# Where the output tiles of a four-layer program stand: later in three phases, earlier in the last one, with row scores of the third layer among its projections

## What is computed

```python
x = x + attn_a(layernorm(x))   # gated slot attention, 16 heads of 128: short convolutions of
                               # q, k, v, w; decays g; a scan over tokens; then
    o = o * rsqrt(mean(o * o, axis=-1) + 1e-5) * norm_w * sigmoid(gate)   # gate = h @ Wg1 @ Wg2 + bg2
    return o.reshape(...) @ Wo
x = x + ffn(layernorm(x))      # causal attention, 16 heads of 128, and 4 experts with top 2
x = x + attn_b(layernorm(x))   # full attention, 16 heads of 16
x = x + ffn(layernorm(x))      # the same weights again
```

## Time and profile before

| | us |
|---|---|
| median of 3 runs | 2605.76 |
| lowest, highest | 2604.42, 2606.11 |
| profiled execution | 2609.29 |
| its span in the trace | 2607.4 |

### The profile page before, as it was taken

How to read it: one execution, slowest core, us unless ns; L and a number is a source line. 1 busy time by engine, 2 the same in 40 slices (tenths; PEclk the granted TensorE clock), 3 DMA queues, 4 the chain that set the end, 5 groups by cost and what they waited for, 6 DMA issues and landing times. The chain is left out here.

```text
span 2607.4 us, 49048 instructions
## 1 busy us (share of the span) xinstructions
PE 2329.5 (89%) x18400; PEld 1615.0 (62%) x18400; DVE 1677.2 (64%) x3286; ACT 1191.4 (46%) x2936; POOL 1100.7 (42%) x1265
## 2 busy tenths in 40 slices
PE   7888888888888888888759999999889989999999
PEld 4577655776557865577635666676533356666685
DVE  7667686677766767677536777742357567777613
ACT  5655455554555545555324555432115535455411
POOL 0477434774347743377525544420130035444300
PEclk9999999999999999999879999998889989999999
DMA  2100001000010000000012000000100030000000
GB/s 63 37 2 3 2 17 37 2 2 2 17 37 2 2 2 17 17 3 2 2 52 74 15 19 19 7 1 1 50 1 1 1 115 19 19 19 13 1 1 17
DMA packets 57640, 46.29 MB, mean 18 GB/s; under 512 B 11576, under 2 KB 50880, under 8 KB 57024
## 3 DMA queue, kind: packets, MB, share of 16 engines
q1 hardware_dynamic: 57408, 43.16, 5.7%
HBM read 42.10 MB, written 1.05 MB: 17 GB/s over the span
## 5 line engine op out<-in xcount | busy, mean ns | idle before, releaser
L1182 DVE SCALAR_TENSOR_TENSOR work<-four,taps,work 128x511 f32<-128x511 f32 (+2 forms) x384 | 285.4, 748 | 101.6 <-ACT work L861 92.0
L1807 POOL TENSOR_TENSOR rot<-q_plain,ropes 128x512 f32<-128x512 f32 x64 | 81.0, 1266 | 577.0 <-ACT q_plain L1838 577.0
L931 ACT ACTIVATE work<-four 128x512 f32<-128x512 f32 x216 | 129.0, 597 | 270.1 <-PE four L690 243.8
L576 PE MATMUL four<-xT,wring 128*128 128x512 f32 x512 | 252.2, 620 | 0.2 <-DVE work L1182 0.2
L741 PE MATMUL four<-work 128*128 128x128 f32 x1536 | 217.2, 286 | 0.0
L1851 ACT ACTIVATE pr<-four,nmaxf 128x512 f32<-128x512 f32 (+3 forms) x256 | 134.0, 525 | 171.2 <-DVE nmaxf L1689 171.2
L1689 DVE TENSOR_REDUCE nmaxf<-four 128x1 f32<-128x512 f32 (+3 forms) x256 | 125.8, 491 | 125.7 <-PE four L1532 121.7
L741 PEld LDWEIGHTS four<-work 128*128 128x128 f32 x1536 | 193.5, 196 | 4.0
L1530 PE MATMUL four<-rot,rot 128*128 128x512 f32 (+3 forms) x512 | 179.0, 445 | 5.2 <-DVE rot L1681 3.6
L1117 POOL TENSOR_TENSOR work<-work 128x256 f32<-128x256 f32 x184 | 146.5, 796 | 77.5 <-DVE work L1263 56.1
L1124 POOL TENSOR_TENSOR work<-work 128x256 f32<-128x256 f32 x184 | 141.9, 771 | 84.0 <-PE bank L775 74.0
(11 more groups left out here) (276 smaller groups left out, 5429.3 us busy)
## 6 DMA issues: line engine op xcount, KB each, us to landing
wqkv<-in_f_wq_dram SPq DMA_DIRECT2D x32, 128.0 KB, 2.2
wqkv<-in_f_wk_dram SPq DMA_DIRECT2D x32, 128.0 KB, 2.4
wqkv<-in_f_wv_dram SPq DMA_DIRECT2D x32, 128.0 KB, 2.3
wo<-in_f_wo_dram SPq DMA_DIRECT2D x2, 2048.0 KB, 11.7
we<-in_f_we_dram SPq DMA_DIRECT2D x4, 1024.0 KB
wring<-in_Wk_dram SPq DMA_DIRECT2D x4, 512.0 KB, 3.8
wring<-in_Ww_dram SPq DMA_DIRECT2D x4, 512.0 KB, 5.5
wring<-in_Wv_dram SPq DMA_DIRECT2D x4, 512.0 KB, 3.9
```

Of the source, the lines that this page charges most:

```text
L576: last = nc.tensor.matmul(unit_bank(i)[:], wring[n % 2][:, c, h * P:(h + 1) * P], k.xT[:, c, b * T:(b + 1) * T], start=(c == 0), stop=(c = ...
L1182: ins = nc.vector.scalar_tensor_tensor(out=cbuf[i % 4][:, n:], in0=unit_bank(i)[:, 0:T - n], scalar=taps[:, {"q": 0, "k": 1}.get(kind, 2), ...
```

## The change

It has four parts, and no arithmetic is changed.

1. **Phases of groups 1 to 3.** For an output tile `turn_y` comes 4 steps after its first step (3 before), `keep_y` 5 (4), `result` 7 (5), `add` 8 (6).
2. **Last group.** Six of its 8 tiles (those whose chunks are complete; `LAST_TILES` orders them first) are issued among the levels of s = 8 and s = 9 (`LATE`, `last_outputs`): `gate` of tile e, `turn_y` of e - 1, `result` of e - 2 at place e. They use banks 0, 2, 3 and other buffers. POOL makes the roots in two parts: 24 of 32 columns at s = 8, j = 0, and 8 after the slots. Two tiles stay behind the slots.
3. **Norm statistics.** `measure` takes `bn_stats` and `bn_aggr` of a tile right after the last addition to it, in the last group of the first layer, in the last expert of the second and at the end of the third. The three blocks that follow lose theirs and wait for a counter.
4. **Third layer.** The four row scores of unit 0 follow the parts 4, 7, 10 and 13 of the projections, their maxima on DVE one part later. The projections move from banks 0 to 3 to banks 4 to 7.

```diff
@@ -144,7 +145,16 @@
+def measure(k, dve, stage, n, t=None):
+    nc, signal = k.nc, k.measured[stage]
+    t = n if t is None else t
+    nc.vector.bn_stats(k.stats[:, t, :], k.x[:, t, :]).then_inc(signal, 1)
+    dve.wait_ge(signal, 2 * n + 1)
+    nc.vector.bn_aggr(k.mean_var[:, t, :], k.stats[:, t, :]).then_inc(signal, 1)
...
+LATE = {(B * CH, j): j - 1 for j in range(1, LEVELS)} | {(B * CH + 1, 0): LEVELS - 1, (B * CH + 1, 1): LEVELS}
+LAST_TILES = [b * CH + c for b in range(B) for c in range(CH - 1)] + [b * CH + CH - 1 for b in range(B)]
+NEARLY = B * (CH - 1)
...
 (PE)
+                def last_outputs(e):
+                    gate(NG, e)
+                    if 1 <= e <= NEARLY:
+                        turn_y(NG, e - 1)
+                    if 2 <= e <= NEARLY + 1:
+                        result(NG, e - 2)
...
-                    t = token_tile(g, i - 3)
+                    t = token_tile(g, i - 4)
                     if t is not None:
                         turn_y(g, t)
                     t = token_tile(g, i)
                     if t is not None:
                         gate(g, t)
-                    t = token_tile(g, i - 5)
+                    t = token_tile(g, i - 7)
                     if t is not None:
                         result(g, t)
...
                     if g == NG:
-                        gate(g, 0)
-                        for t in range(NT):
-                            if t + 1 < NT:
-                                gate(g, t + 1)
-                            turn_y(g, t)
-                            if t:
-                                result(g, t - 1)
+                        turn_y(g, NT - 2)
+                        turn_y(g, NT - 1)
+                        result(g, NT - 2)
                         result(g, NT - 1)
                         break
...
                             if early(g, s, j) is not None:
                                 phase(g + 1, early(g, s, j))
+                            if late(g, s, j) is not None:
+                                last_outputs(late(g, s, j))
...
 (ACT)
-                    t = token_tile(g, i - 4)
+                    t = token_tile(g, i - 5)
                     if t is not None:
                         keep_y(g, t)
...
 (POOL)
+                            if g + 1 == NG and (s, j) == (B * CH, 0):
+                                pool.wait_ge(out_squared, g * SLOTS * HG + NEARLY * HG)
+                                root(NG, by_chunk(ss_o)[:, :, 0:CH - 1], by_chunk(rt_o)[:, :, 0:CH - 1], [P, B, CH - 1, HG])
+                            if late(g, s, j) is not None and late(g, s, j) < NEARLY:
+                                weigh(NG, late(g, s, j))
...
 (DVE)
+                    if g == NG:
+                        dve.wait_ge(x_added, (g - 1) * NT + t + 2)
+                        measure(k, dve, 0, t, m)
...
+                def last_outputs(e):
+                    bias(NG, e)
+                    if 1 <= e <= NEARLY:
+                        scale_y(NG, e - 1)
+                    if 2 <= e <= NEARLY + 1:
+                        add(NG, e - 2)
...
-                    t = token_tile(g, i - 6)
+                    t = token_tile(g, i - 8)
                     if t is not None:
                         add(g, t)
...
 (second layer, DVE, last expert)
+                        if n >= E * NT and rows is None:
+                            dve.wait_ge(y_used, n + 1)
+                            measure(k, dve, 1, t)
...
 (third layer)
+FIRST_ROWS = {4 + 3 * r: r for r in range(CH)}
...
+                    if i in FIRST_ROWS:
+                        pe.wait_ge(c_roped, 2)
+                        score_rows(0, FIRST_ROWS[i])
...
+                    if n - 1 in FIRST_ROWS:
+                        maximum(0, FIRST_ROWS[n - 1])
```

More of the change, by code:

```diff
@@ L169, in then @@
                 dve.wait_ge(k.norm_chain, chain[0])
[L171 to L176 removed]
+            if measured is None:
+                for t in range(NT):
+                    last = nc.vector.bn_stats(k.stats[:, t, :], src[:, t, :])
+                then(last)
+                for t in range(NT):
+                    last = nc.vector.bn_aggr(k.mean_var[:, t, :], k.stats[:, t, :])
+                then(last)
+            else:
+                dve.wait_ge(k.measured[measured], 2 * NT)
             nc.vector.tensor_scalar(k.rstd[:], k.mean_var[:, :, 1], EPS, None, ALU.add).then_inc(k.norm_var, 1)
@@ L1225, in _ @@
                     if g == NG:
-                        bias(g, 0)
-                        for t in range(NT):
-                            if t + 1 < NT:
-                                bias(g, t + 1)
-                            scale_y(g, t)
-                            if t >= 2:
-                                add(g, t - 2)
+                        scale_y(g, NT - 2)
+                        scale_y(g, NT - 1)
                         add(g, NT - 2)
@@ L2196, in _ @@
                     if n < NC_UNITS:
-                        for r in range(1, CH):
+                        for r in range(1, CH) if n else ():
                             maximum(n, r)
```

191 lines of the change are left out of this document (110 added, 81 removed).

## The result

| | before | changed |
|---|---|---|
| median of 4 runs, us | 2605.94 | 2557.40 |
| lowest, highest | 2604.42, 2606.31 | 2552.39, 2561.54 |
| profiled execution, its span | 2609.29, 2607.4 | 2561.54, 2559.8 |

The ratio is 0.9821 with a 95% interval of 0.9802 to 0.9840: 47 us faster (42 to 52). Forecast were 2560.6, or 45.2 us, in a range of 2546 to 2584.

The account below looks back on a forecast made before the run. PE, busy 89% of the span, bounds the kernel with its list plus its waits. Terms -28.5 - 2.7 - 2.45 + 2.7 - 12.4 - 1.8 = -45.2 us, giving 2560.6 us, range 2546 to 2584.

Parts of the forecast that it names:

- Part 1, forecast -28.5: Phases of groups 1 to 3: waits for `scale_y` nearly vanish, those for additions partly stay; 9.5 us gained per group.
- 3 to 6.8 us of waits are left: Phases of groups 1 to 3: of PE's 14.0 us of waits per group, this much remains after the change.
- the `scale_y` was to start ahead of POOL's weighing: In the phases, `scale_y` would start 0.3 us before POOL's weighing, which otherwise makes it 3.61 us in place of 0.68.
- Part 2, forecast -2.7: Last group: six tiles among the levels; its end with statistics at 1350.6 in place of 1353.35, bounds -10 and +15.
- Four steps of the working: Last group: chunk 7's first level +6.8 us, a level 5.6, low clock 3 for the first tile, 4.5 for the last two.
- Part 3, forecast -2.45, +2.7 and -1.8: Norm statistics: second layer's beginning gains 2.45 us, its end loses 2.7, third layer's end and fourth's beginning gain 1.8.
- Part 4, forecast -12.4: Third layer: 17.07 us less 3.9 for row scores and 2.3 for the fourth maximum, plus 1.5 from the clock; bounds -9, -15.
- what the clock gives back behind the transpose: Third layer: without the long idle stretch the clock stays up and the next two steps come 1.5 us earlier.
- Rival 1: Phases: waits for additions replace those for turns, gain 3 us per group in place of 9.5; 2580 us, chance 0.15.
- Rival 2: Last group's levels run at the lower clock, five of them adding 17.5 us; 2578 us, chance 0.12.
- Rival 3: All 14 us of waits vanish in each group and the tail runs at full clock; 2540 us, chance 0.08.
- Rival 5: Most of 32 `scale_y` meet POOL's work, 2.93 us more each; kernel slower, 2619 us from 20 of 32; chance 0.04.

Follow-up runs that it names:

- the weighing in pieces: POOL's weighing of bw cut from two instructions into eight, on the changed kernel with additions first, row scores earlier, no second-layer statistics and unread matmuls: 2528.37 us, ratio 0.9716.
- the warm end: Seven unread matmuls ahead of the last two tiles' turns in the last group, on the changed kernel: 2552.92 us, ratio 0.9809.
- part 4 alone: The kernel before with only the third layer's row scores moved among its projections, and these on banks 4 to 7: 2591.72 us, ratio 0.9958.
- additions first on the old distances: The kernel before with only the addition moved to the head of its step, turn_y 3, keep_y 4, result 5, add 6: 2601.18 us, ratio 0.9990.
- three smaller edits: On the changed kernel: row scores two parts earlier, no second-layer statistics, seven unread matmuls before the last tiles; together with additions first 2538.93 us, ratio 0.9761.

## Why the prediction came out right, point by point

**Part 1, forecast -28.5.** The mechanism was right, the size only in part. From the last projection of group 0 to the first pair of s = 8, three executions without part 1 took 1181 to 1186 us, five with it 1149 to 1158; between the means, 1183.4 and 1153.5, lie 30.0. In the waits, 9.3 + 4.7 became 4.1 + 1.3 + 0.6, which is 8.0 a group and not 9.5; PE's whole idle time fell by 22.7. The other 7.2 us are PE's busy time for the same matmuls, which the forecast had put at nothing; that fewer waits keep the clock up is likely, but not shown apart from the scatter. So that the phases came to what was forecast is partly luck. That "3 to 6.8 us of waits are left" holds (6.0). The reason given for the wait that is left, an addition of the step before, is confirmed by the edit that moves the addition to the head of its step. One point failed: the `scale_y` was to start ahead of POOL's weighing. It still meets it, at the last tile of each phase, and takes 3.21 us (3.61 before); the new wait of 1.3 us at a turn is this one, and the run with the weighing in pieces shows that it held more than that once the additions were out of the way.

**Part 2, forecast -2.7.** This term was mis-sized. From the first pair of s = 8 to the end of the last statistics or addition, before took 75.1 us (1278.23 to 1353.35) and the changed kernel 65.1 (1253.40 to 1318.47): -10.0, the forecast's lower bound. Four steps of the working differ. The first level of chunk 7 came 4.5 us later here, not 6.8, but that is chance: of nine executions with part 2, six with a granted clock of 0.58 or 0.59 up to that level had it 6.2 to 6.7 later, and three with 0.66 to 0.88 had it 4.5 to 4.8 later. POOL's root itself was sized well:

```profile
1255.28 4.15 POOL L1111 TENSOR_TENSOR rt_o<-rt_o,power 128x24 f32<-128x24 f32 x1
...
1303.93 1.63 POOL L1111 TENSOR_TENSOR rt_o<-rt_o,power 128x8 f32<-128x8 f32 x1
```

A level took 5.34 us, not 5.6 (1.3 for five). The first two gates took 1.98 and 1.91 us in place of 1.1, but the first turn already ran at the full clock (0.66), so that 1 to 2 of the 3 us set aside for the first tile weren't due. And the last two tiles did run at half, as forecast, but by the warm end this costs 2.6 us and not 4.5. These are 2.3 + 1.3 + 1 to 2 + 1.9 = 6.5 to 7.5 of the 7.3 us that are to be told of. Two other executions of the same stretch were 2 us slower (74.7 in place of 72.8 us to the second layer's first projection), so -8 is met as well, and there the first of the four steps was right: what stays mis-sized is 4 to 5 us, in the levels and in what the lower clock costs.

**Part 3, forecast -2.45, +2.7 and -1.8.** Nothing is mis-sized by more than a microsecond. ACT at the beginning of the second layer, to be held against the earlier trace rows:

```profile
1319.97 1.28 ACT L1951 ACT_TABLE_LOAD   x1 [7.89 <-PEq L144]
1321.26 0.22 ACT L1951 ACTIVATE roots<-roots 128x16 f32<-128x16 f32 x1
```

The root starts 2.8 us after the last statistics; before it was 5.2 after the last addition: -2.44. The table load is last now, as forecast. In the fourth layer, from the start of the third layer's last addition to the root, it is 4.44 and 2.68, -1.76. At the end of the second layer the middle statistics cost 2.0 us by four executions with them and ten without (1.7 by the profiled pair), against 2.7; additions come every 1.06 us and not every 1.16. That the loads hide the norm of the third layer was right.

**Part 4, forecast -12.4.** From first projection to transpose 69.4 us before (69.3 to 69.8 in three of four other executions without part 4, 68.1 in the fourth) and 59.7 to 60.2 where v kept its clock: -9.4, forecast -10.9. Two sizes were off. The first is the price of the row scores. They were counted at 3.9 us in all, 0.96 to 1.14 each for PE alone; in the loop a part with row scores takes 3.83 us in place of 2.58 (by the starts of DVE's products at `L2242`: 1868.95 and 1872.78, against 1857.36 and 1859.94), so 1.25 each and 5.0 in all. The fourth maximum is then 17.07 - 5.0 - 9.4 = 2.7 us, near the 2.3 that were forecast. In the profiled execution and in the run of part 4 alone the clock fell behind that wait, which the forecast had not priced; there it is -6.3 and -8.2. The second is what the clock gives back behind the transpose. The 1.5 us for the next two steps are as forecast (5.6 became 4.15), but the forecast stopped there. To the next transpose 19.6 us (19.6 to 19.8 in four of five executions without part 4, 17.4 in the fifth) became 15.9 in every one with it, -3.7. So part 4 is worth some 13 us where v keeps its clock and 10.0 in the profiled pair; that its sum is near 12.4 comes from two errors that cancel.

**The sum.** In the profiled pair the terms are -24.8 for the phases (the same point of the last slots stands at 1278.23 and 1253.40), -10.0, -2.4, +1.7, -6.3 - 3.7 and -1.8, in all -47.3, against 47.7 between the two profiled executions. That this is near the forecast's 45.2 is in good part chance: a last group 7 us and middle statistics 1 us better stand against phases 3.7 and a third layer 2.4 worse in this execution.

**Rivals.** Rival 1 (additions take over, 0.15): no, 4.1 us and not 11; but the run with additions first on the old distances shows that such taking over is how this loop behaves. Rival 2 (the last group's levels at the lower clock, 0.12): no, the clock is 1.00 throughout. Here waits of 1.4 to 1.6 us in every level did not throw PE back, with PE busy for 22.2 of the 29.9 us from 1268.00 to 1297.93. The Trainium skill, page "TensorE: Matmul & The Clock Gate", section "HAM oscillation — how this bites in real kernels", describes waits for data between bursts of matmuls that bring the half rate each time. Those are longer than the waits of a level, so the prediction applied the section to a case that it doesn't describe; behind the idle stretch of 6.74 us the granted clock was 0.50, and there the trace agrees. Rival 3 (waits vanish whole): no, 6 us a group stay. Rival 4 (late weights): no, the first projection at 1326.16 waits for ACT. Rival 5 (`scale_y` meets POOL, 0.04): the mechanism is real but at one `scale_y` in eight, as the forecast said; over all 32 the mean is 1.10 us. Cutting POOL's instruction showed it: 3.21 became 1.07. The Trainium skill, page "SBUF — State Buffer", section "Who interferes with whom", has an exclusive lock for the length of an instruction; the trace agrees, with `scale_y` ending 0.55 us behind the POOL instruction that it met, whether that one took 3.6 or 1.04 us.

## What to carry to other kernels

Where two engines of nearly equal load wait for each other in a software pipeline, first ask which of the waits is the one of distance (a step too short); shortening another wait in the same ring gives nothing until that one is cured, as the same edit shows, with nothing on the old distances and 13 us on the new ones. After that, put the short instruction that frees a single buffer at the head of its step, ahead of the long ones, and cut long POOL instructions where VectorE works beside them with both inputs in SBUF: the first gave 13 us (6 to 21) and the second 10.6, and with three smaller edits the kernel stands at 2528.4 us. A wait of PE that goes can give back more than its own length, since the matmuls behind it keep the full clock. Size a short stretch behind a wait from several executions, since the clock behind it is not the same in each; one trace gave 63.1 us where others gave 60.

## What the hardware showed that was not expected

- The granted clock after one and the same wait of 3.25 us ahead of the same 24 matmuls fell in two executions (8.22 and 7.13 us) and not in three others (5.45). Ahead of a turn a wait of 3.06 us was followed by the lower clock in 8 of 9 places of three executions. After a wait of 1.5 us ahead of the 24 matmuls, in four executions, it didn't fall.
- In chunk 7's levels PE was busy for 74% of the time, with waits of 1.4 to 1.6 us, and kept 2.4 GHz. Before the change the same levels, with PE busy for a third and no wait over 1.22 us, had 0.62: the length of a wait alone doesn't tell the clock.
- Matmuls whose result nobody reads hold the clock: seven of 128 x 512 in a gap of 6.7 us took 6.17 us and saved 2.6 behind it.
- A VectorE instruction of 0.68 us took 3.21 beside a POOL instruction of 3.6, and 1.07 beside one of 1.04; both ended 0.55 us behind it.
- POOL's power took 4.15 us on 24 columns and 1.63 on 8, with 5.41 on 32: 0.157 us a column and 0.37 for the start.
